# Grouped attention of a seven-stage kernel: from phases per sequence to steps of one quad of heads

## The reference

```python
q = (query @ Wq).reshape(b, sq, 32, 32).transpose(0, 2, 1, 3)
k = (key @ Wk).reshape(b, sk, 8, 32).transpose(0, 2, 1, 3)    # key = value = context
v = (value @ Wv).reshape(b, sk, 8, 32).transpose(0, 2, 1, 3)
k, v = repeat each head 4 times
probs = softmax(einsum('bhqd,bhkd->bhqk', q, k) * 32 ** -0.5)
out = einsum('bhqk,bhkd->bhqd', probs, v).transpose(0, 2, 1, 3).reshape(b, sq, 1024) @ Wo
```

## Time and profile before

| | us |
|---|---|
| median of 3 runs (3369.56 to 3383.47) | 3380.32 |
| the profiled execution | 3379.05 |
| its span, first to last instruction | 3377.4 |
| PE busy in the span | 2917.9 (86%) |
| DVE, ACT, POOL busy | 2090.3, 1129.3, 462.0 |
| granted TensorE clock, mean | 0.930 |

### The profile page before, as it was taken

The page is one execution under the profiler, slowest core; times in us unless marked ns, Lnnn a source line. Parts: engine busy times, 40 slices in busy tenths (PEclk is TensorE's granted clock), DMA queues, the critical chain, the costliest instruction groups (busy, mean ns, idle before and its releaser), DMA issues. The chain is left out here.

```text
span 3377.4 us, 55656 instructions
## 1 busy us (share of the span) xinstructions
PE 2917.9 (86%) x20468; PEld 2057.5 (61%) x20468; DVE 2090.3 (62%) x3684; ACT 1129.3 (33%) x2348; POOL 462.0 (14%) x540
## 2 busy tenths in 40 slices
PE   7999999999964999785999999999778888847888
PEld 4666566566642788663565555665567677635664
DVE  5544544554447667554665655665578888946774
ACT  3333343333331233222544344544333223211222
POOL 0111011011022000000221122211222322200000
PEclk9999999999987999977999999999888988867999
DMA  6100110010034455353333222331410000035441
GB/s 229 43 31 12 42 43 31 11 42 31 5 104 158 133 141 142 94 185 130 113 123 124 74 87 94 117 106 56 154 38 23 18 18 18 22 100 183 155 142 45
DMA packets 102177, 288.77 MB, mean 86 GB/s; under 512 B 33352, under 2 KB 56552, under 8 KB 92432
## 3 DMA queue, kind: packets, MB, share of 16 engines
q1 hardware_dynamic: 70928, 166.09, 14.9%
q0 software_dynamic: 22160, 103.47, 9.5%
q10 hardware_dynamic: 8848, 16.10, 1.8%
HBM read 242.57 MB, written 43.04 MB: 85 GB/s over the span
## 5 line engine op out<-in xcount | busy, mean ns | idle before, releaser
L2043 PE MATMUL bank<-ffn_qT,ffn_wgu 128*128 128x112 bf16 x4096 | 244.4, 230 | 57.3 <-DVE ffn_gs L2226 48.8
L2043 PEld LDWEIGHTS bank<-ffn_qT,ffn_wgu 128*128 128x128 fp8e4 x4096 | 240.3, 108 | 63.6 <-issue 61.1
L1462 DVE TENSOR_REDUCE latent_nmax<-bank 112x1 f32<-112x487 f32 x128 | 85.2, 666 | 270.2 <-PE bank L1327 262.7
L2173 POOL TENSOR_TENSOR ffn_h<-ffn_sl,ffn_us 128x448 f32<-128x448 f32 x64 | 136.7, 2135 | 406.2 <-ACTq L2128 227.7
L1288 PEld LDWEIGHTS bank<-latent_hT,latent_wq 128*128 128x128 f32 x1536 | 180.4, 195 | 9.5 <-issue 9.1
L1661 PE MATMUL bank<-grouped_kT,grouped_qT 128*112 128x375 f32 x512 | 178.8, 492 | 6.2 <-ACT grouped_probs L1782 5.9
L1288 PE MATMUL bank<-latent_hT,latent_wq 128*128 128x112 f32 x1536 | 179.6, 278 | 0.0
L1251 POOL TENSOR_SCALAR latent_probs<-latent_probs,latent_rsum 112x487 f32<-112x487 f32 x128 | 88.1, 688 | 658.6 <-DVE latent_rsum L1467 658.6
L2127 ACT ACTIVATE ffn_sl<-ffn_gs,ffn_sgu 128x112 f32<-128x112 f32 x256 | 78.4, 376 | 292.6 <-DVEq L2228 292.5
L1815 POOL TENSOR_SCALAR grouped_probs<-grouped_probs,grouped_rsum 112x375 f32<-112x375 f32 x256 | 147.2, 594 | 173.4 <-DVE grouped_rsum L1893 173.4
L1266 PE MATMUL bank<-latent_wv,latent_hT 128*125 128x384 f32 (+1 forms) x512 | 168.3, 490 | 0.0
(11 more groups left out here) (398 smaller groups left out, 5902.4 us busy)
## 6 DMA issues: line engine op xcount, KB each, us to landing
grouped_raw<-L_weights POOLq DMA_DIRECT2D x24, 2048.0 KB, 8.5
points_spread<-numbers SPq DMA_DIRECT2D x32, 912.0 KB
codes<-grouped_code SPq DMA_DIRECT2D x24, 512.0 KB, 4.3
latent_hT<-ctxT SPq DMA_DIRECT2D x8, 1500.0 KB, 6.8
plain_ctxT<-ctxT POOLq DMA_DIRECT2D x8, 1500.0 KB, 16.5
plain_ctx<-ctx POOLq DMA_DIRECT2D x8, 1500.0 KB, 34.7
grouped_ctxT<-ctxT SPq DMA_DIRECT2D x8, 1500.0 KB, 12.2
latent_xy<-planes SPq DMA_DIRECT2D x8, 1024.0 KB, 8.4
```

What stands on the lines that cost most here:

```text
L2043: mm = pe.matmul(ahead.tile(t)[:, i * Q:(i + 1) * Q], wgu[:, u0 + f // 4, c:c + P], qT[:, k, :], start=(k == 0), stop=(k == KC - 1))
L2173: pool.tensor_tensor(h[:, G * j:G * j + G, :], sl[:, j % 2], us[:, j % 2], ALU.mult).then_inc(h_ready, 1)
```

## The change

The stage becomes one sequence of steps `g` from -8 to 66, one quad each, written out without a loop. Step `g` has the scores of quad `g` and the transposes and the product of quad `g - 1`. `PLAN` says what stands between them on every engine: 8 rows, one for each quad of sequence `b`, with the keys, `z`, queries and values of sequence `b + 1`, the result `y` of sequence `b - 1` and the weight tiles of sequence `b`, in the places `first` (behind the scores), `middle` (between the second and the third `pT` tile) and `last` (ahead of the product). `("k0", 0)` is the first half, 4 of the 8 matmuls, and `("k0", 1)` the second.

The scores of a head use its own 32 rows of `qT` and `kT` as operands, and `kT` has no copies and no zeros any more. `qT`, `kT`, `v` and `oT` have two buffers, `probs` has two instead of three, `probsT` one instead of two; `z` is a buffer of its own, loaded by a transfer of its own. `k`, `y`, `q` and `v` all use bank 6, `w` bank 7, `pT` banks 4, 5, 4, and each quad's product bank 5, from which ACT copies it at once. The first part of the weights' rounding is split in `measured` (four maxima over 1024) and `scaled` (the rest), which stand in certain steps. All transfers are started by SP.

```diff
+    N = B * QUADS
+    BEGIN, END = -QUADS, N + 3
+    PLAN = [([("k0", 0)], ["w0"], [("k0", 1), "w1"]),
+            ([("y0", 0)], ["w2"], [("y0", 1)]),
+            ([("y1", 0)], ["w3"], [("y1", 1), "zT", "w4"]),
+            ([("k1", 0)], ["w5"], [("k1", 1)]),
+            ([("q0", 0)], ["w6"], [("q0", 1), "w7"]),
+            ([("q1", 0)], [], [("q1", 1), "w8"]),
+            ([("v0", 0), ("v0", 1)], ["w9"], ["qT", "w10"]),
+            ([("v1", 0), ("v1", 1)], ["w11"], [("v2", 0), ("v2", 1)])]
...
-            for s in range(2):
-                sp.dma_start(x[:, s, :], x_in[s]).then_inc(x_loaded[s], 16)
-                sp.dma_start(cT[:, s], A["ctxT"][s].rearrange("(k p) n -> p k n", p=P)).then_inc(ctx_loaded[s], 16)
...
+            normal(0)
+            context(0)
+            for n in range(2):
+                sp.dma_start(x[:, n, :], x_in[n]).then_inc(x_loaded[n], 16)
+            context(1)
+            weights(0)
+            weights(1)
+            normal(1)
...
-                                pe.matmul(turns.tile(t)[0:Q, 0:CTX], qT[:, m, :], kT[:, j, m // 4, :], start=True, stop=True)\
+                    r = slice(j * HD, (j + 1) * HD)
+                    pe.wait_ge(turns.free(t), turns.count(t, 0))
+                    pe.matmul(turns.tile(t)[0:Q, 0:CTX], qT[r, n % 2, m, :], kT[r, n % 2, m // 4, :], start=True, stop=True)\
+                      .then_inc(turns.full(t), 1)
...
+            for g in range(BEGIN, END):                  # PE
+                b, (first, middle, last) = step(g)
+                ahead = 0 <= g - 1 < N
+                if 0 <= g < N:
+                    scored(g)
+                do(first, b)
+                if ahead:
+                    turned(g - 1, 0)
+                    turned(g - 1, 1)
+                do(middle, b)
+                if ahead:
+                    turned(g - 1, 2)
+                do(last, b)
+                if ahead:
+                    output(g - 1)
...
+            for g in range(BEGIN, END):                  # ACT
+                if 0 <= g < N:
+                    exponents(g)
+                if g % QUADS == 1 and b + 1 < B:
+                    norm.root(act, 0, b + 1)
+                do(first, b)
+                do(middle, b)
+                if ahead:
+                    last_tile(g - 1)
+                do(last, b)
+                if ahead:
+                    output(g - 1)
...
+            for g in range(BEGIN, END):                  # DVE
+                b, (first, middle, last) = step(g)
+                r = g % QUADS
+                if 0 <= g < N:
+                    maxima(g)
+                rounded_for(middle, b)
+                if 0 <= g < N:
+                    sums(g)
+                if 0 <= g - 1 < N:
+                    tiles(g - 1)
+                if r == 0 and b + 1 < B:
+                    dve.wait_ge(z_loaded, 16 * (b + 2))
+                    norm.statistics(dve, z[:], 0)
+                if r == 1 and b + 1 < B:
+                    norm.scale(dve, z[:], z[:], 0, b + 1).then_inc(z_ready, 1)
+                if r == 0 and b == B:
+                    numbered()
+                if r in (2, 5) and 0 <= b < B:
+                    scaled(3 * b + (1 if r == 2 else 2))
+                if r in (1, 2) and 1 <= b <= B:
+                    result(b - 1, r - 1)
+                rounded_for(last, b)
+                if r in (1, 4) and 0 <= b < B:
+                    measured(3 * b + (1 if r == 1 else 2))
+                if r == 6 and b + 1 < B:
+                    measured(3 * b + 3)
+                if r == 7 and b + 1 < B:
+                    scaled(3 * b + 3)
```

More of the change, by code:

```diff
@@ L1550, in grouped_attention @@
-        order += [(("y", 0, i), 6 - i) for i in range(2)]
-        turns = Turns(banks, order, B)
-        block = ctx.enter_context(nc.Block())
[L1554 to L1561, removed]
-                for s in range(2):
-                    sequence(p, s, False)
-            for s in range(2):
-                sequence(PAIRS - 1, s, s == 1)
+        z_loaded = s_.sem("z_loaded")
@@ L1609, in _ @@
                 pe.wait_ge(early.loaded[n], 16)
[L1611 to L1615, removed]
-                mm.then_inc(turns.full(t), 1)
[L1618 to L1626, removed]
-                    mm.then_inc(turns.full(t), 1)
@@ new lines, in do @@
+            def do(items, b):
+                for item in items:
+                    t = at(item, b)
+                    if t is None or (not isinstance(item, str) and item[1] == 0):
+                        continue
+                    kind, n, i = t
+                    if kind == "w":
+                        slot = n % 2
+                        if i == 0 and n >= 2:
+                            act.wait_ge(code_stored[slot], n // 2 * 32)
+                        act.wait_ge(turns.full(t), turns.count(t, 0))
+                        o = code[:, slot, :].rearrange("p (k i c) -> p k i c", i=4, c=P)[:, :, i, :] if n % 3 < 2 else \
@@ new lines, in rounded_for, with maxima @@
+            def rounded_for(items, b):
+                for item in items:
+                    t = at(item, b)
+                    if t is not None and t[0] == "w":
+                        rounding(t[1], t[2])
+            def maxima(g):
+                for j in range(4):
+                    t = ("S", g, j)
+                    dve.wait_ge(turns.full(t), turns.count(t, 0))
+                    dve.tensor_reduce(nmax[:, g % 2, j:j + 1], turns.tile(t)[0:Q, 0:CTX], AX, ALU.max, negate=True).then_inc(max_ready, 1)
@@ new lines, in sums, with tiles @@
+            def sums(g):
+                dve.wait_ge(exp_ready, g + 1)
+                dve.reciprocal(rsum[:, g % 2, :], rsum[:, g % 2, :]).then_inc(sum_ready, 1)
+            def tiles(g):
+                if g >= 1:
+                    dve.wait_ge(turns.full(("o", g - 1)), turns.count(("o", g - 1), 0))
+                for k in range(2):
+                    t = ("pT", g, k)
+                    dve.wait_ge(turns.full(t), turns.count(t, 0))
+                    dve.tensor_copy(pT[:, k, :, :], turns.tile(t)[0:CT, 0:4 * Q].rearrange("p (j q) -> p j q", j=4)).then_inc(turns.free(t), 1)
+                dve.drain().then_inc(pT_ready, 1)
@@ L1920, in _ @@
-            every(dve, sequence)
+            for g in range(BEGIN, END):
+                b, (first, middle, last) = step(g)
+                r = g % QUADS
+                if 0 <= g < N:
+                    maxima(g)
+                rounded_for(middle, b)
+                if 0 <= g < N:
+                    sums(g)
+                if 0 <= g - 1 < N:
+                    tiles(g - 1)
[5 more added lines that the diff above has]
+                if r == 0 and b == B:
+                    numbered()
+                if r in (2, 5) and 0 <= b < B:
[9 more added lines that the diff above has]
+                    scaled(3 * b + 3)
```

498 lines of the change are left out of this document (234 added, 264 removed).

## The result

The changed kernel takes 3323.26 us (median of 4 runs, 3318.99 to 3326.07), the kernel before 3381.89 beside it (4 runs, 3369.56 to 3384.72). The ratio is 0.9834, interval 0.9809 to 0.9858: 1.7% faster. The forecast was 3310 (3290 to 3330), with 3270 to 3362 as the range that holds 8 in 10.

The account below looks back on a forecast made before the run. PE's work was taken to bound the stage (95.3 of 102.1 us a sequence), DVE second. Terms -94.9 + 44.3 - 8 - 10.5 = -69 took 3379.05 us to 3310, forecast 3290 to 3330, 8 in 10 within 3270 to 3362.

Parts of the forecast that it names:

- four scores: Scores of a quad on PE: 0.8 us instead of 2.52, as four matmuls on different rows overlap.
- PE's work in a sequence: Steady sequence: PE's 95.3 us become 81.5, since cheaper scores save 13.8.
- PE's waits in a sequence: Steady sequence: 6.6 us of new waits for DVE, about as many as today, whose three go.
- seven sequences: Seven sequences at 88.5 us each: 619.5 against 714.4, so -94.9.
- last sequence and tail: Last eight steps 76 us, then tail 24.5: together 100.5 against 56.2, so +44.3.
- first context lands, from its issue: Start of the stage: first context, now ahead in SP's queue, 8 us earlier, so -8.
- from there to first score: Start, first key matmul to first score: PE has 37.3 us instead of 47.8, so -10.5.
- the first rival: Quad scores do not overlap: half serial 1.6 us, 3347 (chance 0.1); serial 2.52, 3393 (same 0.06, slower 0.08).
- The walk along DVE's queue: Steady sequence, step by step: where DVE's order makes PE wait, mainly step 1's lateness 4.1 and step 5 1.8; 6.6 us.
- The second rival: Steady sequences: DVE becomes the bound, its waits double, +46 us, 3356; chance 0.16 together with a late transfer.
- the third, a late transfer: SP's one queue: a transfer 4 us late once a sequence, 3338; chance 0.16 together with DVE as bound.

Follow-up runs that it names:

- The third experiment: Changed kernel with DVE's scan, division and multiplication of a weight unit cut into pieces of 1024 columns, spread over the steps: 3279.23 us, ratio 0.9697.
- the experiment with POOL: Changed kernel with the 2 MB weight transfers started by POOL again instead of SP: 3340.93 us, ratio 0.9899.
- The experiment with banks of its own: Changed kernel with the first sequence's keys, queries and values in banks 0 to 5, and ACT's root ahead of its first keys' copy: 3318.76 us, ratio 0.9807.

## Why the prediction was right, and where it was off

By its own terms, in stage time:

| term | forecast | measured |
|---|---|---|
| four scores | 0.8 us | 0.83 |
| PE's work in a sequence | 81.5 | 81.7 |
| PE's waits in a sequence | 6.6 | 6.7 |
| seven sequences | -94.9 | -90.8 |
| last sequence and tail | +44.3 | +50.8 |
| first context lands, from its issue | -8 | -9.9 |
| from there to first score | -10.5 | +2.2 |
| sum | -69 | -47.7 |

*Scores.* The nearest row, the product's four column tiles at 3.1 times, carried over to four row tiles: 2.52 / 0.83 is 3.04. The first records of the four start 7 ns after one another, so the first rival (0.3 us apart) is out. The Trainium skill, "TensorE: Matmul & The Clock Gate", Part 3, had 3.07, so 0.82; the trace agrees. The drain in the Trainium skill's "TensorEngine Tiling (Array Packing)", Key Properties, has no price of its own here: with a switch on either side, the work behind the four scores starts 0.83 after them. That is 0.20 more than the 0.63 of a full overlap. And the two full-row matmuls put ahead of row scores take 1.44 until these begin (2089.62 to 2091.06 in that kernel's trace), 0.18 more than their 1.26. Whether a drain is in either was not separated.

*Waits.* The walk along DVE's queue found the right places: step 2 16.9 (forecast 15.7), step 5 12.8 (12.1), maxima 4.8 into step 2 (4.5). It left out one wait, 1.0 for ACT's copy of the turned `q` in step 6 (9.84 instead of 8.2 plus a little), and had those for DVE too high, 6.6 for 5.7; that the sums agree to 0.1 is luck. (The 95.3 that the 81.5 starts from is a slip: 667.9 / 7 is 95.4.) The third experiment shows that these waits were DVE's blocks: 5.7 us a sequence go when they are cut. The second rival (DVE's waits double) fell, and so did the third, a late transfer: no wait of DVE from 1715 to 2254 ends with a transfer, and the experiment with POOL has the same steps.

*The last sequence and the tail.* 83.4 for the eight steps instead of 76, 23.6 for the tail instead of 24.5. Steps 0 and 2 are 1.2 and 1.4 above the walk. In step 5, behind PE's wait of 5.36 for DVE, the granted clock drops (0.69 from 2300 to 2340), and steps 5 to 7 are 15.7, 8.95 and 8.5 for 14, 7.1 and 6.5, with the product at 1.35 instead of 0.78. All durations of the forecast were from rows at full clock, in a stretch that was to leave PE idle for a third of the time.

*The start* is the step that failed: "From there to the first score PE has k, zT, q, v, qT: 37.3 us" (its own terms, 10.3, 0.8, 13.9, 3 x 3.5 and 0.8, even give 36.3). The sum took PE's work alone. It missed that with everything in bank 6 each phase waits until ACT has emptied it, and that `z`'s root on ACT stands behind the first keys' copy: 7.4 us of waits, and another 5 at half the clock. The experiment with banks of its own gives 38.32, with 1.8 of it from the first keys at half the clock and a wait of 0.6 at the end, so the work was sized rightly and the rest is the waits and the clock. The bounds of the context's landing, 12 earlier and 4 later, had no row; it came 9.9 earlier, and no run shows that one queue moves less. In the steady steps the same bank is harmless, since a quad's work lies between its users.

The profiled executions differ by 60.1 us where 69 were forecast, though the stage itself gained 21 less than forecast: 11.6 of the 60 lie behind the stage, in unchanged code. That the time was met more closely than the terms is luck. The terms were right on what pays, the seven sequences, and on how much PE and DVE have to do in them.

## What to carry to other kernels

When work is interleaved to keep the busiest engine fed, first write out the order of the second engine too, and cut its long blocks until none is longer than the slack of what stands behind it; here that gave nearly as much again as the change. A saving on an engine is worth something only where that engine sets the cycle: the same 1.7 us a quad were worth 81 to 87 us in one order and less than nothing in the other. Price the fill and the drain of a pipeline apart from its steady part, with their own buffer waits, and at the lower clock.

## What the runs showed of the hardware

Four float32 matmuls of 32 rows by 375 columns, each on its own rows, take 0.83 us together; one over 128 rows takes 0.63 (2.52 / 4). The granted clock does not follow PE's busy share alone: 9.3 of 10 us busy with work on 32 rows ran at 0.50, 8.9 of 10 with scores over 128 rows at 1.00, and 1.26 us of full-row matmuls a quad raised the quads' clock from 0.81 to 0.96. Doubled scores on 32 rows, with transposes and products, ran at 1.00 later in the same block, PE busy for 14 of 14 us. In the changed kernel row-tiled scores stand between projections over all rows, and the clock is 1.00 in the steady sequence shown and 0.97 over seven. And the order in which transfers stand in one queue decided when a 1.5 MB transfer landed, 8.2 us or 18.1, with the same bytes ordered within a few microseconds.
